# A graph layer on one core: TensorE's weighing products of a group moved from behind the third turn of a round to behind the first

## What is computed

```python
h_e = jnp.einsum('nf,hfd->hnd', x, W_e)
h_r = jnp.einsum('nf,hfd->hnd', x, W_r)
diff = h_r[:, dst] - h_r[:, src]
score = s_src + s_dst + jnp.einsum('hed,hd->he', diff, a_dif) \
      + jnp.einsum('hed,hd->he', jnp.abs(diff), a_abs) \
      + jnp.einsum('hed,hd->he', hr_src * hr_dst, a_prd)
alpha = leaky_relu(score).T          # one number per edge and head
att = softmax of alpha over the edges that share a src
out = segment_sum(att[:, :, None] * h_e[:, dst], src)
```

## Time and profile before

| | |
|---|---|
| median of 3 runs | 1358.79 us (1356.1 to 1359.14) |
| the profiled execution, first to last instruction | 1481.0 us |
| what lies around that span | not recorded; the trace gives no time of its own beside the span |
| mean granted TensorE clock | 0.934 of full speed |
| busy: PE, DVE, ACT, POOL | 86%, 73%, 49%, 51% |
| instructions of `reduce` (L967) | 672 products, 672 weight loads |
| scoring stage in the trace | about 215 to 775 us |

### The profile page before, as it was taken

One profiled execution on the slowest core, in us unless ns is written; L12 is line 12 of the kernel. 1 busy time (PEld: TensorE's weight loads), 2 busy tenths in 40 slices (PEclk: granted clock), 3 DMA queues, 4 the chain that ended last, 5 costly groups with the idle time before them and its releaser, 6 DMA issues. The chain is left out here.

```text
span 1481.0 us, 23733 instructions
## 1 busy us (share of the span) xinstructions
PE 1266.5 (86%) x6722; PEld 818.5 (55%) x6797; DVE 1088.2 (73%) x2240; ACT 730.7 (49%) x1218; POOL 755.9 (51%) x860
## 2 busy tenths in 40 slices
PE   6999967989999999989985878888788873999985
PEld 2555533545555545545543567776676662777763
DVE  8998875999989898898988667666676778212126
ACT  5555425888888888888881000000000045555541
POOL 1201035666666666666617666565655451555651
PEclk9999977999999999999995899998989896999998
DMA  8233358888888888888837777776776565343478
GB/s 238 95 115 129 128 182 255 274 255 272 276 273 261 283 263 279 261 269 266 275 99 204 235 256 248 226 246 223 262 226 213 173 227 200 121 135 128 134 256 309
DMA packets 141842, 324.67 MB, mean 219 GB/s; under 512 B 30178, under 2 KB 46294, under 8 KB 141610
## 3 DMA queue, kind: packets, MB, share of 16 engines
q0 software_dynamic: 62816, 212.87, 45.6%
q1 hardware_dynamic: 76842, 109.42, 21.7%
q10 hardware_dynamic: 2080, 1.05, 0.3%
HBM read 257.35 MB, written 65.93 MB: 218 GB/s over the span
## 5 line engine op out<-in xcount | busy, mean ns | idle before, releaser
L1288 PE MATMUL m_ps<-msg,hot 128*128 128x260 f32 x1344 | 335.5, 408 | 64.0 <-issue 60.2
L1288 PEld LDWEIGHTS m_ps<-msg,hot 128*128 128x128 f32 x1344 | 272.0, 204 | 127.5 <-issue 84.4
L1139 POOL DMA_INDIRECT big<-he_d,target x234 | 230.1, 983 | 138.7 <-DVE msg L1212 71.9
L1011 ACT ACTIVATE big<-big,raw_a 128x512 f32<-128x512 f32 x336 | 273.6, 814 | 11.2
L935 PE MATMUL gs_ps<-big,hot_t 128*128 x944 | 264.2, 386 | 10.7 <-issue 5.3
L1009 ACT ACTIVATE big<-d_ps 128x512 f32<-128x512 f32 x336 | 195.7, 583 | 108.4 <-PE d_ps L948 83.1
L794 DVE TENSOR_TENSOR big<-big 128x512 f32<-128x512 f32 x336 | 229.4, 683 | 14.0 <-ACT big L1011 7.3
L1212 DVE TENSOR_TENSOR msg<-big 128x512 f32<-128x512 f32 x336 | 211.9, 683 | 0.8
L765 POOL DMA_INDIRECT x_sb<-table_d,target x150 | 149.7, 998 | 106.2 <-PE d_ps L948 75.2
L1155 ACT COPY big<-m_ps 128x520 f32<-128x520 f32 x20 | 11.8, 591 | 357.1 <-PE m_ps L1288 178.1
L790 DVE TENSOR_TENSOR x_sb<-x_sb,gs_ps 128x512 f32<-128x512 f32 x204 | 138.9, 681 | 40.7 <-PE lin_ps L939 18.5
(11 more groups left out here) (349 smaller groups left out, 1749.0 us busy)
## 6 DMA issues: line engine op xcount, KB each, us to landing
big<-early_d SPq DMA_DIRECT2D x84, 256.0 KB
early_d<-x_sb SPq DMA_DIRECT2D x51, 256.0 KB
x_sb<-local_d SPq DMA_DIRECT2D x84, 128.0 KB
early_d<-big SPq DMA_DIRECT2D x33, 256.0 KB
big<-in_L_ffn_W_dram SPq DMA_DIRECT2D x16, 512.0 KB
big<-pairs_d SPq DMA_DIRECT2D x6, 1024.0 KB, 9.9
table_d<-big POOLq DMA_DIRECT2D x10, 520.0 KB, 3.3
both_d<-big POOLq DMA_DIRECT2D x10, 520.0 KB, 4.2
```

The source lines that it names most:

```text
L1011: act.activation(uv[:, j, c, :], ab[:, j, c, :], ACT.Identity, bias=raw[:, 0, c:c + 1], scale=raw[:, 1, c:c + 1]).then_inc(ur, 1)
L1139: pool.indirect_dma_start(g[:, r, t, :, :, :].rearrange("p c h d -> p (c h d)"), None, he_d, bass.IndirectOffsetOnAxis(ap=k["target"][:, q ...
L1288: last = pe.matmul(m_ps[:, bass.ds(slot[t], 1), j, 0:HEADS // 2 * HW].rearrange("p a f -> p (a f)"), hot[:, r, t, :], halves[:, r, t, j, : ...
```

## The change

`reduce(n - 2)` is issued behind the first turn of round `n` instead of behind the third. The loop is otherwise the same, and so are all waits and all other engines' programs.

```diff
@@ on_tensor of score_edges
                         fetch(n, t, blocks[t])
                     if 1 <= n <= G:
                         turn(n - 1, t)
-                    if t == 2 and n >= 2:
+                    if t == 0 and n >= 2:
                         reduce(n - 2)
```

## The result

The changed kernel takes 1531.05 us (median of 4 runs, 1527.16 to 1533.78), the kernel before 1357.91 us in the same comparison. The ratio is 1.127 (95% interval 1.125 to 1.129): 173 us slower. The profiled execution ran 1533.13 us and spans 1531.0, so it is as long as the other runs; the first recording of the kernel before was 122 us longer than its runs.

A forecast was written before the change was run, and what follows sets the result against it. DVE was nearest to the bound, PE just behind; after the move both wait for each other in a 7.82 us loop. 1358.79 + 150 for the rounds + 1 for the end gave 1510 us, range 1450 to 1580.

The forecast's parts named there:

- The wait opens in every round: PE before the moved `reduce`: the once-met wait for DVE's `times(n-2,3)` is open every round, 1.5 to 2 us.
- The new round, counted round the loop: Scoring loop between PE and DVE: 0.69 + 0.06 + 1.87 + 4.73 + 0.47 = 7.82 us a round, against 6.39.
- The loop through ACT, covered by 0.1 us: ACT's fourth quarter ends 6.49 us after `reduce`, DVE gets to it at 6.60, so ACT adds nothing.
- What it gives back: Most of DVE's 0.59 us of idle time a round goes; only one idle of 1.93 us is left.
- The round of the kernel before without recording: Unrecorded scoring round of 5.80 to 5.86 us instead of 6.39; the rise is 116 to 164 us, 150 taken.
- The lateness of 0.78 us: `subtract` starts 2.65 us after `reduce` beside gathers, not 1.87; at most 63 us more, counted as nothing.
- The end of the stage: Behind the loop, the last group's turns start after the moved `reduce`: about 1 us more.
- The granted clock: Rival, chance 0.20: PE's idle 1.5 to 2 us a round lowers TensorE's clock in scoring; 42 us more, 1552 us.
- The signs named beforehand: Scoring stage: right if `reduce` stand 7.8 us apart; wrong if shorter wait, rounds under 7 us, or clock under 1.
- No change, by the rule of the fullest engine: Rival, chance 0.03: engine loads alone decide and the move leaves them unchanged, so 1359 us.
- Absorbed: Rival, chance 0.05: PE's spare 0.71 us a round takes up most of its wait; 24 us more, 1383 us.
- faster: Rival, chance 0.02: `reduce` waits for nothing and DVE wins back 0.59 us a round; 48 us at most, 1311 us.

The follow-up runs named there:

- e3: Against the changed kernel, the products behind the first turn are those of group n-3 instead of n-2, with one more round at the end: 1376.09 us.
- e7: Against the changed kernel, 6 or 12 small products that nobody reads are given out ahead of `reduce` to fill PE's wait: 1504.20 us.
- e4: Against the changed kernel, DVE does `times(n-2,3)` ahead of `subtract(n,0)` instead of behind it: 1487.27 us.
- e8: The kernel before, unedited, recorded a second time: it ran 1357.14 us and the recording spans 1355.0 us.
- e2: Against the kernel before, the weighing products stand behind the fourth turn instead of the third: 1354.15 us over 11 runs, 0.997.
- e1: Against the kernel before, the weighing products stand behind the second turn instead of the third: 1387.43 us, 1.019 times.

## Why the prediction was right

The forecast was 1510 us, slower, in a range of 1450 to 1580; measured 1531. The mechanism is the one that was forecast; one term was left out. Step by step:

- *The wait opens in every round.* Right: PE's L967 waits for DVE L794 in every round, 1.7 us on average, within the 1.5 to 2 that were named; in ordinary rounds it is 1.41, just below. e3 shows that this input costs nearly all of the loss, and the place at most a tenth.
- *The new round, counted round the loop.* The bare round of 7.35 us was measured at 7.34. With the other work it was reckoned at 7.82; e7, whose clock does not fall, has 7.72 on average, so the 0.47 us of other work was 0.1 too much.
- *The loop through ACT, covered by 0.1 us.* Right, by e4: it comes out when DVE's loop is shortened by 0.6 us, and the round falls by 0.10.
- *What it gives back.* DVE waits only for its fetch after the products, 1.92 us against the 1.93 reckoned.
- *The round of the kernel before without recording.* Bounded by 5.80 and 6.39; the rise of 150 us that was chosen stands for 5.97, and e8 shows 5.95. The 150 was picked between 116 and 164, not worked out, so that it comes within 2 us of 7.82 less 5.95 over 81 rounds is in part luck. Had the sum been made against the span alone, the rise would have been 117 us. The lateness of 0.78 us in the earlier trace rows did not stay in the loop, as was assumed: the changed kernel's recording has 1.87 us in its ordinary rounds.
- *The end of the stage.* Reckoned as 1 us more, measured 4.
- *The granted clock.* This is the term that was mis-sized, by being left out of the forecast and made a rival with 0.20. It fell, and the loss is 26.9 us (e7), against the rival's 42. The two are not alternatives: the loop came true in full and the clock on top. The measured terms are (7.72 - 5.95) x 81 = 143 us for the loop, 26 for the clock in the rounds and 4 for the end, 173 in all. The rival's share of one fifth was read from the message stage of the first recording, whose clock of 0.90 does not come back in e8; the changed kernel's 0.95 over its rounds is a tenth of the time at 1.2 GHz. It also expected the fall from the pause of every round; it comes only in the longer ones, behind 19 of the 30 pauses of 1.96 to 2.73 us.
- *The signs named beforehand.* Two of those that were to show the forecast wrong did appear, a granted clock under 1 in the stage and a wait before L967 under 1.5 us in ordinary rounds, and the rounds are 8.04 us apart on average instead of 7.8. The first is the missing term; the second did not shorten the round.
- *No change, by the rule of the fullest engine.* Wrong here: the loads are the same, and the time is 13% longer. The rule holds for the kernel before and for e2, where PE and DVE are full, and says nothing of a loop in which both wait.
- *Absorbed, and faster.* Neither occurred; e1 shows what a part absorbed looks like, 28 us instead of 173.

The Trainium skill (page "TensorE: Matmul & The Clock Gate", section "HAM oscillation — how this bites in real kernels") tells of a loop whose DMA waits of some 3 to 5 us put the clock down in every pass. The prediction took it to make the falling clock the likeliest case, but the pauses that it tells of are longer than any in these rounds. The trace agrees with it in that the clock goes down again and again in the rounds with the longer pauses, with 0.90 granted over 285 to 400 us; it does so at 1.96 to 2.73 us already, and never in the ordinary rounds.

## What to carry to other kernels

Before a waiting instruction is moved forward on one engine, look at what stands between its input's maker and the same round's first handover on the other engine: if the other engine needs something from behind the moved instruction, the two orders form a loop, and its length is the sum of both, however free the engines are. The first slots of distance are worth far more than the later ones: against the kernel before, the products cost 173, 28, 0 and -4 us behind the first, second, third and fourth turn. And a trace longer than its runs should be recorded again before rounds are read from it.

## What the runs showed of the hardware

The same program was recorded once with a span of 1481.0 us and once with 1355.0, its runs at 1358. In the first, other engines often went on late after PE's products (2.65 us from `reduce` to `subtract` in the earlier trace rows, 1.87 where nothing is late), and the granted clock in the message stage was 0.90 instead of 1.00; what was different is not known. Filling TensorE's pauses with products that nobody reads took 27 us off; the same filling where pauses were shorter took nothing off, since part of it came onto the path. The clock fell behind all ten pauses of 2.67 to 2.73 us and behind nine of twenty of 1.96 to 2.14, and a round with a fall was some 1.5 us longer (10.2 against 8.66 us). Eight weighing products of 512 columns took 1.00 us to the next fetch, of 256 columns 0.57.
